# A graph layer's kernel: second buffers for the last stage's output and features, a test sum placed earlier, and one copy of counts placed earlier

## The reference, cut to what matters

```python
# x: 12500 x 128; src, dst, edge_type_9: 200000 edges, sorted by dst
src_h = h[src] @ W_msg.T + b_msg
msg = src_h + edge_embed[clip(edge_type, 0, 8)]
messages = segment_sum(msg, dst, 12500)
gi = messages @ W_ih.T + b_ih ; gh = h @ W_hh.T + b_hh
r = sigmoid(i_r + h_r) ; z = sigmoid(i_z + h_z) ; n = tanh(i_n + r * h_n)
h_new = (1 - z) * n + z * h
out = layernorm(x + h_new)
```

## Time and profile before

| quantity | value |
|---|---|
| median of the runs | 1158.32 us |
| the profiled execution: its own time, its span | 1161.39 us, 1159.6 us |
| busy: PE, DVE, ACT, POOL | 987.2, 858.9, 634.4, 861.1 us |
| POOL's indirect DMAs for the sparse tiles | 88 from x, 680 from x_split |
| granted TensorE clock, mean | 0.945 |

### The profile page before, as it was taken

How to read it: one execution, slowest core, us unless ns; L and a number is a source line. 1 busy time by engine, 2 the same in 40 slices (tenths; PEclk the granted TensorE clock), 3 DMA queues, 4 the chain that set the end, 5 groups by cost and what they waited for, 6 DMA issues and landing times.

```text
span 1159.6 us, 33091 instructions
## 1 busy us (share of the span) xinstructions
PE 987.2 (85%) x13301; PEld 818.9 (71%) x13301; DVE 858.9 (74%) x2652; ACT 634.4 (55%) x1217; POOL 861.1 (74%) x811
## 2 busy tenths in 40 slices
PE   5667888888888988889899899899989989979963
PEld 2245767777767767778788788788878878868741
DVE  8636586777778768887788788788877868778453
ACT  4743243564565446656666567565756746656342
POOL 7747777777777777777777777777787777777740
PEclk8966899998999999999999999999999999989986
DMA  8876223333333333333333333333333333333330
GB/s 262 239 243 195 55 53 87 87 92 78 102 87 86 89 87 87 88 91 93 97 88 92 94 90 92 89 96 92 97 83 89 102 93 92 96 87 100 98 82 25
DMA packets 95896, 118.01 MB, mean 102 GB/s; under 512 B 20091, under 2 KB 81399, under 8 KB 95736
## 3 DMA queue, kind: packets, MB, share of 16 engines
q0 software_dynamic: 36800, 76.33, 25.4%
q1 hardware_dynamic: 57080, 37.80, 11.2%
q10 hardware_dynamic: 1856, 1.68, 0.5%
HBM read 99.74 MB, written 16.00 MB: 100 GB/s over the span
## 4 chain that ended last, share of the span: by engine, by line
PE 39%; DVE 16%; POOL 12%; DMA 11%; issue 9%; ACT 7%; SPq 5%; DVEq 0%; ACTq 0%
PE psf L985 15%; POOL xg L507 12%; PE psb L970 6%; DMA xg<-x_split,idx 5%; PE pAB L927 5%; SPq L415 5%; DVE ohk L758 5%; PE pAB L913 3%; ACT mem L1092 3%; PE psg L952 3%; PE psg L948 2%; DMA out<-arena 2%; PE pAB L930 2%; DVE ohk L768 1%; DMA arena<-in_x 1%
## 5 line engine op out<-in xcount | busy, mean ns | idle before, releaser
L507 POOL DMA_INDIRECT xg<-x_split,idx x680 | 736.5, 1083 | 210.7 <-issue 179.8
L985 PE MATMUL psf<-mem 128*128 128x128 f16 x7644 | 585.4, 222 | 13.9 <-ACT mem L1092 13.9
L1092 ACT CAST mem<-psb 128x428 f16<-128x428 f32 x832 | 398.3, 520 | 320.3 <-PE psb L970 317.0
L985 PEld LDWEIGHTS psf<-mem 128*128 128x128 bf16 x7644 | 504.9, 99 | 60.6 <-ACT mem L1092 19.7
L970 PE MATMUL psb<-ohk,ohl 128*128 128x107 bf16 (+3 forms) x1801 | 385.9, 259 | 41.9 <-DVE ohk L768 26.2
L758 DVE TENSOR_TENSOR ohk<-iota,prm 128x432 bf16<-128x432 f16 (+3 forms) x421 | 279.8, 665 | 65.3 <-PE psb L970 63.9
L970 PEld LDWEIGHTS psb<-ohk,ohl 128*128 128x128 bf16 x1801 | 160.2, 100 | 75.3 <-DVE ohk L768 33.2
L758 DVE TENSOR_TENSOR ohl<-iota,prm 128x512 bf16<-128x512 f16 x421 | 175.6, 417 | 0.0
L952 PE MATMUL psg<-ohs,xg 128*128 128x56 bf16 (+9 forms) x2040 | 106.9, 196 | 39.6 <-DMA xg<-x_split,idx 33.3
L790 DVE TENSOR_TENSOR mem<-mem,psg 128x112 f32 (+10 forms) x192 | 56.7, 296 | 91.8 <-PE psg L957 86.1
L952 PEld LDWEIGHTS psg<-ohs,xg 128*128 128x128 bf16 x2040 | 87.8, 97 | 50.6 <-DMA xg<-x_split,idx 40.1
(11 more groups left out here) (124 smaller groups left out, 796.9 us busy)
## 6 DMA issues: line engine op xcount, KB each, us to landing
xg<-x_split,idx POOLq DMA_INDIRECT x680
x_split<-mem SPq DMA_DIRECT2D x24, 384.0 KB
xb<-in_xT SPq DMA_DIRECT2D x49, 128.0 KB
arena<-in_xN SPq DMA_DIRECT2D x49, 128.0 KB
arena<-in_x SPq DMA_DIRECT2D x24, 256.0 KB, 6.4
out<-arena SPq DMA_DIRECT2D x35, 128.0 KB
out<-arena SPq DMA_DIRECT2D x208, 8.0 KB
xg<-in_x,idx POOLq DMA_INDIRECT x88
```

What stands on the lines that cost most here:

```text
L507: pool.indirect_dma_start(out=xg[:, p % RING, :] if split else xg32(p % RING), out_offset=None, in_=x_d if split else x, in_offset=bass.In ...
L985: ins = pe.matmul(psf[:, q % 2, 0:FB], xs[0:kk, h, c, :], Bb[q % 2][0:kk, NT + h, :], start=(h == 0 and c == 0), stop=(h == HI - 1 and c = ...
L1092: act.copy(Bb[q % 2][:, :, n:n + MOST], psb[:, bank % NB, 0:MOST * HC].rearrange("p (d h) -> p h d", h=HC)).then_inc(S["s_eb"], 1)
```

## The change

There are four edits.

- `yo` becomes a pair, `yos`: the old place in `arena` and a new tile `spill`, used in turn. `s_o` becomes a pair of semaphores, and `ln(i)` waits for the stores of block `i - 2` in place of `i - 1`.
- `xb` gets two halves, and `s_x` becomes a pair: the load for block `i` waits for `hh(i - 2)` in place of `hh(i - 1)`.
- PE's sum of the tests moves from behind the 27 steps of the split to behind step `t` = 21.
- In `schedule()`, the `end` mark and the `cn` of the last block move to directly behind the last `GA`.

```diff
+SUM_AT = 21
@@ schedule()
-            slots = [[(s, done, b) for s in slot if s != "zero" or b >= CB0] for slot in SLOTS]
+            slots = [[(s, done, b) for s in slot if (s != "zero" or b >= CB0) and (s != "cn" or done != ahead)]
+                     for slot in SLOTS]
...
         chunks[min(1, len(chunks) - 1)].append(("GA", g))
+        if g == GROUPS - 1:
+            ahead = done if len(main) == 1 else None
+            chunks[min(1, len(chunks) - 1)] += [("end",)] + [("cn", done, b) for b in main if len(main) == 1]
...
-    items.append(("end",))
@@ stored(i)
-    return 16 * sum(STORES[:i + 1])
+    return 16 * sum(STORES[i % 2:i + 1:2])
@@ buffers
-        xb = sb("xb", [P, BN])
+        xb = sb("xb", [P, 2, BN])
...
-        yo = arena[:, 5 * BN:6 * BN].rearrange("p (s h) -> p s h", s=2)
+        spill = sb("spill", [P, BN])
+        yos = [t.rearrange("p (s h) -> p s h", s=2) for t in (arena[:, 5 * BN:6 * BN], spill[:, :])]
@@ SP, finish()
-                    if i:
-                        sp.wait_ge(S["s_hh"], i)
-                    sp.dma_start(xb[:, :], xT[:, b * BN:(b + 1) * BN]).then_inc(S["s_x"], 16)
+                    if i > 1:
+                        sp.wait_ge(S["s_hh"], i - 1)
+                    sp.dma_start(xb[:, i % 2, :], xT[:, b * BN:(b + 1) * BN]).then_inc(s_x[i % 2], 16)
...
-                sp.wait_ge(S["s_o"], stored(NBLK - 1))
+                for i in (NBLK - 2, NBLK - 1):
+                    sp.wait_ge(s_o[i % 2], stored(i))
@@ DVE, ln
-                    if i:
-                        v.wait_ge(S["s_o"], stored(i - 1))
+                    yo = yos[i % 2]
+                    if i > 1:
+                        v.wait_ge(s_o[i % 2], stored(i - 2))
@@ PE, the steps of the split
-            pe.wait_ge(S["s_bad"], 1)
-            pe.matmul(psg[0:1, 2 * P:2 * P + J + 2], one[:, :], badc, start=True, stop=True,
-                      skip_group_check=True).then_inc(S["s_sum"], 1)
+                if t == SUM_AT:
+                    pe.wait_ge(S["s_bad"], 1)
+                    pe.matmul(psg[0:1, 2 * P:2 * P + J + 2], one[:, :], badc, start=True, stop=True,
+                              skip_group_check=True).then_inc(S["s_sum"], 1)
@@ PE, hh
-                    pe.wait_ge(S["s_x"], 16 * (i + 1))
+                    pe.wait_ge(s_x[i % 2], 16 * (i // 2 + 1))
```

More of the change, by code:

```diff
@@ L161, in schedule @@
     first, main = list(range(CB0)), list(range(CB0, NBLK))
-    done, spent, active, late, added = 0, 0.0, [], None, 0
+    done, spent, active, late, added, ahead = 0, 0.0, [], None, 0, None
     def pick(g, top):
@@ L380, in gnn_kernel @@
                  "s_bi s_em s_cn s_used s_oh s_grp s_acc s_ok s_kd s_eb s_fd s_toh s_tr s_sl s_main "
-                 "s_e18 s_wp s_wc s_x s_xn s_hh s_pm s_rz s_t2 s_n s_y s_mv s_sd s_ln s_xc s_p1 s_xe s_p2 s_xl s_xw s_nid s_o").split()
+                 "s_e18 s_wp s_wc s_xn s_hh s_pm s_rz s_t2 s_n s_y s_mv s_sd s_ln s_xc s_p1 s_xe s_p2 s_xl s_xw s_nid").split()
         S = {n: sem(n) for n in names}
         s_g = [sem(f"s_g{i}") for i in range(RING)]
+        s_o = [sem(f"s_o{i}") for i in range(2)]
+        s_x = [sem(f"s_x{i}") for i in range(2)]
         s_xd = [sem(f"s_xd{i}") for i in range(4)]
@@ L414, in store @@
                     n, p = NODES[n0 + k * RUN], k * RUN % P
-                    sp.dma_start(out[n:n + RUN, :], yo[p:p + RUN, k * RUN // P, :]).then_inc(S["s_o"], 16)
+                    sp.dma_start(out[n:n + RUN, :], yo[p:p + RUN, k * RUN // P, :]).then_inc(s_o[i % 2], 16)
             elif b < NBLK - 1:
-                sp.dma_start(out[n0:n0 + BN, :].rearrange("(s p) h -> p s h", s=2), yo[:, :, :]).then_inc(S["s_o"], 16)
+                sp.dma_start(out[n0:n0 + BN, :].rearrange("(s p) h -> p s h", s=2), yo[:, :, :]).then_inc(s_o[i % 2], 16)
             else:
-                sp.dma_start(out[n0:n0 + P, :], yo[:, 0, :]).then_inc(S["s_o"], 16)
-                sp.dma_start(out[n0 + P:N, :], yo[0:N - n0 - P, 1, :]).then_inc(S["s_o"], 16)
+                sp.dma_start(out[n0:n0 + P, :], yo[:, 0, :]).then_inc(s_o[i % 2], 16)
+                sp.dma_start(out[n0 + P:N, :], yo[0:N - n0 - P, 1, :]).then_inc(s_o[i % 2], 16)
         block = ctx.enter_context(nc.Block())
@@ L910, in final @@
                         pe.wait_ge(S["s_wc"], 1)
-                    pe.wait_ge(S["s_x"], 16 * (i + 1))
+                    pe.wait_ge(s_x[i % 2], 16 * (i // 2 + 1))
                     for s in range(2):
-                        ins = pe.matmul(pAB[:, s, H:4 * H], xb[:, s * P:(s + 1) * P], whh[:, :], start=True, stop=False,
+                        ins = pe.matmul(pAB[:, s, H:4 * H], xb[:, i % 2, s * P:(s + 1) * P], whh[:, :], start=True, stop=False,
                                         skip_group_check=True)
```

## The result

The changed kernel takes 1129.26 us in the median of four runs (1127.97 to 1134.09) against 1158.31 us for the kernel before (1157.09 to 1162.80). The ratio is 0.975 with a 95% interval from 0.971 to 0.979. The forecast was 1130.8 us. The profiled execution took 1128.02 us, its span is 1126.0 us.

The account below looks back on a forecast made before the run. POOL's back-to-back gather stream was taken as the bound; 7.95 us from an earlier stream (5.0 + 2.95) and 19.5 in the tail made 27.5, taking 1158.32 to 1130.8 us. Own range 1125 to 1135, full range 1123 to 1141.

Parts of the forecast that it names:

- What bounds: Sparse part: POOL issues gathers back to back, 1.38 us each, from 77.17 to about 1102 us, and sets the pace.
- The head: Start of the kernel: the earlier sum of the tests starts POOL's gathers 5.0 us earlier, at 72.2 us; bounds 0 and 5.8.
- The second output buffer in the body: Block loop: `ln` no longer waits for the block before; POOL's one long slot wait goes, 2.95 us; bounds 0 and 2.95.
- the early waits: Nine waits of `ln` for stores ahead of 930 us: worth 0, since the gathers hide them; a rival counted 33.9 us, chance 0.03.
- a risk of 6.6 us: Body, a rival: DVE, no longer waiting, crowds POOL and lengthens gathers by 6.6 us, giving 1137.4 us; chance 0.07.
- The prediction's own sign of being wrong: Gather stream: a mean gather more than 0.01 us from 1.08 us, or POOL waiting long for slots again.
- The tail: Last blocks: the idles of 6.28 and 4.06 us ahead of `su` go; 19.5 us gained, end at 1132.1 us.
- Group 190 to 191: Tail on PE: 13.75 us less 6.28 of idle and 1.73 for the full clock gives 5.74 us.
- Group 191 to `hh`: Tail on PE: 2.21 us plus 0.28 for the copy, then a new wait of 0.6 us for features; `hh` at 1117.4.
- The third rival: Tail: its idle returns at the `xb` load or ACT tables, leaving 7.95 and about half of 19.5 us; 1140.6 us, chance 0.06.
- `hh` to the end: End of the tail: `hh` 1.56 us, then `su` at once at full clock, 13.09 us from there to the end.
- the 4.06 us: Tail: PE's idle ahead of `su` of place 48, behind the count copy on DVE; expected to go entirely.

Follow-up runs that it names:

- e6: Unchanged copy of the changed kernel, run while the kernel before took 1459 to 1496 us; ratio to the kernel before 0.989 [0.982, 0.996].
- e9: Changed kernel with the feature load ahead of the stores and the sum at step 20, not 21; 1122.80 us against 1161.44 for the kernel before, ratio 0.968.
- e1: Changed kernel, but `ln` of places 1 to 31 waits again for the stores of the block just before; 1478.77 us against 1495.66 for the kernel before.
- e2: Changed kernel, but `ln` of places 32 to 48 waits again for the stores of the block just before; ratio to the kernel before 0.996 [0.992, 1.000].
- e4: Changed kernel with `end` and the last `cn` put back behind `ln` of place 47; ratio to the kernel before 0.994 [0.990, 0.998].
- e7: Kernel before with only the second output buffer; one `xb`, sum and last copy late as before; ratio to the kernel before 0.994 [0.990, 0.997].
- e5: Changed kernel with the feature load of block `i + 1` issued ahead of the stores of block `i - 2`; ratio to the kernel before 0.988 [0.980, 0.995].
- e8: Kernel before with only the sum of the tests moved to step 21; ratio to the kernel before 1.002 [0.998, 1.006].

## Why the prediction was right, and where it was off

**What bounds.** Right for the condition that was forecast: POOL's stream ran without a slot wait over 0.3 us, and PE was back on the gathers' heels. Where PE and ACT bind, as in e6, this reading fails, and the change is worth 20 us of 1494 (e6) in place of 29 of 1158.

**The head.** Forecast 5.0, measured 4.22 us. The step from the sum to the turns was read rightly: the turns start 6.0 us after PE's sum in the kernel before and 6.1 us after it in the changed one. But the prologue ran 0.8 to 1 us later in this execution: step 21 ended at 61.89 us and not at 60.89, the tests at 56.32 and not at 55.53. The dependence itself is shown by e9, where one step less gave 1.47 us. There the turns follow the split with no idle between them, so a still earlier sum would bring nothing more.

**The second output buffer in the body.** The slot wait went, 2.95 us, and PE's late stretch too. That the early waits are worth 0 was argued and is not shown: the rest of the stream became 10.15 us shorter, and the runs that put these waits back fell into the other condition. Five facts bear on it.

- The mean gather is 1.071 us in the changed kernel and 1.069 in e9, against 1.083 before, which makes 8 to 10 us over 680 gathers.
- From restart to last gather the stream took 1028.80 and 1028.60 us in the two profiles without these waits, so the shorter stream is no accident of one of them.
- Some 4.3 us of the difference between the profiles are not in the medians, which would leave about 6.
- But beside e9 the kernel before had a median of 1161.44 us, that of its profile here, and the medians differ by 38.6 us, like the spans of the two profiles (38.2 us, of which 10.35 lie in the rest of the stream). That speaks against a freak of the single profile of before.
- Gather by gather, the 751 from the restart on took 9.6 us less than in the kernel before. 7.9 us of that fall on the 218 that ran, in the kernel before, during one of the nine early waits or within 30 us behind it. During the waits a gather took 0.947 us, in the 30 us behind them 1.119, against 1.071 for the same gathers in the changed kernel. That points at the bursts of DVE's work after its waits, but does not show it: the difference of a gather between the two profiles scatters by 0.31 us, which by an estimate makes 4.6 us by chance over 218, and against e9's gathers only 5.5 us fall there.

I had priced the effect of DVE on the gathers with the wrong sign as a risk of 6.6 us. So 6 to 10 us are open: either DVE's waits, and the bursts after them, lengthened gathers, or executions differ by that much. The prediction's own sign of being wrong was a mean gather more than 0.01 us from 1.08; at 1.071 it stopped just short of that, and the last gather came at 1101.75 us where it said about 1111.

**The tail.** From group 190 to the end 23.5 us were forecast (1108.6 to 1132.1), 27.5 measured. Three terms were mis-sized. Group 190 to 191 took 6.37 us, not 5.74: `su` was taken at the full clock because PE comes to it straight from `hh`, but that `hh` itself ran at the low clock (2.90 us), and `su` took 2.12 us. Group 191 to `hh` took 4.76, not 3.1: the new wait for features was named, but sized at 0.6 us where `hh` ended up 1.8 us behind `t2`, because the sixteen stores took 8.78 us on SP, not 7.40, and group 190 started 0.35 us behind the end of `yt` of place 46, where the forecast had it 1.5 to 2.1 us behind. It was to start when its rows landed; it started when DVE's `GA` was done. Since e1, with the same code there, held the queue for 7.37 us, the longer stay is variation and not an effect of the change. The third rival had named this wait; it cost a few us of the tail and not half of it. And `hh` to the end took 16.4 us, not 14.65: after that idle the clock was back at its low level. The granted clock in these stretches of the changed kernel:

```profile
1100.00:1104.00 4.00, 4.00 (x7) 2.11 (x7) 1.38 (x5) 1.20 (x1) 2.08 (x3) 0.53 0.36 88
1104.00:1109.60 5.60, 1.83 (x20) 1.11 (x19) 3.01 (x8) 2.30 (x3) 0.00 (x0) 1.00 0.21 45
1109.60:1114.60 5.00, 4.98 (x10) 2.58 (x10) 1.54 (x8) 1.58 (x2) 0.00 (x0) 0.66 0.30 85
```

(the columns after the window are its length, then busy us and instructions of PE, PEld, DVE, ACT and POOL, the granted clock, the DMA share and GB/s). It is 0.53 in 4 us behind group 190, 1.00 while PE is mostly idle, and 0.66 when the last `hh` and `su` run. In e9, where `hh` follows 1.71 us of idle and not 3.43, it stays at 1.00 from 1103 to 1113 us.

**The copy and the second feature buffer.** The copy was priced inside the 4.06 us that went; e2 shows that price where `ln` still waits for stores, and e4 that beside the wait for features alone its place is worth nothing. The second `xb` was forecast at 0 in this form, and e7 agrees. e5 and e9 show what held it back: its load stood in the wrong place of the queue, and moved ahead of the stores it takes 3.3 us off the tail. Whether one `xb` would do with that order was not run.

**Sum.** 27.5 us forecast, 29.05 measured by the medians. The total is nearer than its parts, and that is luck: between the profiles the tail gave 3.2 us less and the head 0.8 less than forecast, the stream 10.15 more, and 4.3 us of the profiles' difference are not in the medians. Without the 6 to 10 us of the stream that were put at 0, the changed kernel would have taken 1135 to 1139 us, at or above the end of the forecast's own 1125 to 1135.

## What to carry to other kernels

When a stream of gathers sets the pace, price first the stalls behind its end and those from which an engine cannot catch up before it. A stall elsewhere is hidden as a wait, but do not put it at 0 before you have compared the gathers around it: here the stream became 10 us shorter when such waits went, and why stayed open. A second buffer helps only if the queue lets its transfer start: look for what is issued ahead of it, above all many small stores, and put the load first. An idle of PE in a serial tail can be paid twice, once as idle and once as the low clock behind it: the last `su` took 2.77 us behind 3.43 us of idle and 1.45 us behind 1.71 us.

## What the runs showed of the hardware

- The kernel before, on the chip with the same number, took 1461.85 us beside e5 and 1161.44 us beside e9. In the slower condition PE was idle for 121 us at two lines (e6) with no releaser in the profile, and the mean gather was shorter, 1.048 us in e8 against 1.083 us in the first condition.
- Sixteen stores of 8 KB occupied SP's queue for 7.37 us (e1) to 8.78 us (the changed kernel), with 7.40 us in the kernel before and 8.28 us in e9; a load queued behind them waited that long.
- TensorE's granted clock rose to 1.00 while PE was nearly idle (1104.0 to 1109.6 us, busy 1.83 us), and was 0.66 when it had work again behind 3.43 us of idle; behind 1.71 us in e9 it stayed at 1.00.
